# Freeing the accumulator banks of two kinds of fill earlier in the slot, and moving a ScalarE cast, in a fused cross-attention and spectral feed-forward layer

## The chip, the cores and the metric

The kernel runs on one core of one Trainium2 chip. The core has TensorE (PE, which multiplies matrices and turns tiles, and writes its results to eight PSUM banks), VectorE (DVE), ScalarE (ACT), GpSimd (POOL) and SyncE (SP, which here only issues DMAs). Each engine works through its own instructions in the order in which they are written, and engines wait for one another through semaphores. The metric is the time of one execution on the device in microseconds (us).

## The reference

Two sequences of 2048 tokens with 512 channels go through one attention layer over 128 context tokens and one feed-forward layer in the frequency domain.

```
def attention(decoder_output, encoder_output, mask, ...):      # 16 heads of 32 channels
    q = decoder_output @ wq_w + wq_b ;  k = encoder_output @ wk_w + wk_b ;  v = encoder_output @ wv_w + wv_b
    score = einsum('bhqd,bhkd->bhqk', q, k) / sqrt(32) * mask
    score = where(score == 0, -1e9, score)
    context = einsum('bhqk,bhkd->bhqd', softmax(score), v)
    return context @ wo_w + wo_b
def ffn(x, w_real, w_imag, bias):
    return real(ifft(fft(x) @ complex(w_real, w_imag))) + bias
x = x + attention(layernorm(x), ctx_1024, mask, ...)
x = x + ffn(layernorm(x), w_freq_real, w_freq_imag, bias)
```

## The kernel before

The spectral layer is folded into one real 512x512 matrix `M` while the kernel starts up. Matrices are split into a high and a low float16 part (`h` and `l`), and a product is made of three float16 matmuls.

**Chunks, slots and fills.** The 4096 tokens are 16 chunks of 256. For each chunk there are four steps of attention, one for each group of four heads, so 64 steps. All engines run a written-out software pipeline of *slots*: slot `v` (`V0` = 2 up to 79) holds the work of step `v` and, behind it by some slots, the later stages of earlier steps. In the text `r` is `v % 4`, and a slot with r = 1 is called an r1 slot. On DVE a slot begins with `mask_mul(v)` (scores times mask, read from the score banks), and then has `zero_to_neg(v)` and `least(v)` (the row minimum). GpSimd turns the minimum into the exponent's bias. ScalarE makes the exponentials of step v-1 in its slot `v`, in two halves, with `copy_pt` (the copies of the turned weights, which PE made by transposing the exponentials of step v-2) between them. PE runs `weigh` (weights times values, in even slots), `turn` (the transposes), then the slot's fills, then `scores(v+1)`, then late fills.

**Fills** are the matmul groups that share the three PSUM banks `G`. Fill number `n` uses bank `n % 3`, and PE may begin it only when fill `n-3` has been freed: `pe.wait_ge(g_free, n - 2)`. DVE raises `g_free`, one count a fill, strictly in the order of the fills' numbers, at the end of its `lo(n)`. The kinds of fill that matter here:

- `QQ`: half of a chunk's query projection, 24 matmuls. ScalarE casts the high part (`qh`, line 683), then DVE takes the low part (`ql`, line 862) and frees the bank. QQ with half 0 stands at the end of r3 slots, half 1 at the end of r1 slots.
- `R`: the reciprocals of the softmax sums, turned by four transposes, at the end of even slots. ScalarE copies them out (`rec`, line 725) at the head of the next slot; DVE only has to raise `g_free` with an empty instruction (line 847).
- `ST`: the token statistics of a coming chunk, two small transposes (line 462). ScalarE copies them out (`srow`, line 649), DVE again only raises `g_free` on line 847.
- `WO` (r0 and r1 slots) and `FF` (r2 and r3 slots): output projection and feed-forward, 12 matmuls each, read by DVE alone (lines 869 and 875).
- `U` and `M`: the pieces of the folded matrix, only in slots 4 to 11, with copies `od` on ScalarE (line 664) and sums on DVE (827, 832). `fold` on DVE (line 946) adds up pieces of the spectral matrix in slots 4 and 5.

A slot's fills in the plan are `mid` ones, ahead of the scores, and `late` ones behind them. ScalarE and DVE deal with the late fills of slot v-1 in slot `v`, as `held`. Both do so near the end of the slot's work: DVE behind `least(v)`, ScalarE behind both halves of the exponentials and `ctx_hi`:

```
for n in held + mids:
    lo(n)
```

In the steady stretch the order of fills is FF, QQ (r3 slot), WO, R, ST (r0 slot), WO, QQ (r1 slot), FF, R (r2 slot). So the QQ of the r1 slot takes the bank of the R of the r0 slot, and the ST takes the bank of the QQ of the r3 slot.

Of the kernel before, what the change touches and what calls it, by code (L numbers as in the profile page):

```python
# [17 lines left out]
NC = NB * S // CH  # L18
NS = 4 * NC
V0, V1 = 2, NS + 16  # L20
VS = 9
VP = 4
LAST = ("FF", NC - 1, 1)
NEG = 1e9
MASK_SCALE = 1e-9 / 32.0 ** 0.5 / 8.0
# [11 lines left out]
def plan():  # L37

    fills, slots, held = [], {}, []
    lead = [("W1", 0), ("CT", 0), ("CT", 1), ("K", 0), ("ST", 0), ("Q", 0, 0), ("Q", 0, 1), ("S", 0),
            ("W1", 1), ("Q", 0, 2), ("S", 1), ("K", 1), ("Q", 0, 3), ("ST", 1), ("Q", 1, 0), ("S", 2),
            ("Q", 1, 1), ("Q", 1, 2), ("Q", 1, 3)]
    front = []
    for f in lead:
        if f[0] == "S":
            front += [("S", f[1], 0), ("S", f[1], 1)]  # L50
        else:
            front.append(("G", len(fills)))
            fills.append(f)
    early = {
# [3 lines left out]
    }  # L58
    queries = {2: (2, 0), 4: (2, 1), 5: (3, 0), 6: (3, 1)}
    for v in range(V0, V1):  # L60
        c, r = divmod(v, 4)
        mid = {
            0: [("WO", c - 2, 0)],
            1: [("WO", c - 2, 1)],
            2: [("FF", c - 3, 0)],
            3: [("FF", c - 3, 1)],
        }[r]
        mid = [f for f in mid if 0 <= f[1] < NC] + early.get(v, [])
        if mid == [LAST]:
            mid = [LAST, (*LAST, "right")]  # L70
        late = []
        if v % 2 == 0 and 0 <= v - 4 < NS:
            late.append(("R", (v - 4) // 2))
        if v % 4 == 0 and 3 <= v // 4 + 2 < NC:
            late.append(("ST", v // 4 + 2))
        if v in queries:
            late.append(("QQ",) + queries[v])
        elif v >= 7 and v % 2 == 1 and (v + 9) // 4 < NC:
            late.append(("QQ", (v + 9) // 4, (v + 9) % 4 // 2))
        base = len(fills)  # L80
        fills += mid + late
        mids = list(range(base, base + len(mid)))
        lates = list(range(base + len(mid), len(fills)))
        items = []
        if v % 2 == 0 and 0 <= v - 4 < NS:
            items += [("PV", (v - 4) // 2)]
        if 0 <= v - 2 < NS:
            items += [("PT", v - 2, 0), ("PT", v - 2, 1)]
        items += [("G", n) for n in mids]
        if 0 <= v + 1 < NS:  # L90
            items += [("S", v + 1, 0), ("S", v + 1, 1)]
        items += [("G", n) for n in lates]
        slots[v] = (items, held, mids)
        held = lates
    return fills, front, slots


def stats_slot(c, t):
# [7 lines left out]
def hi_slot(c):  # L106
    return 5 if c == 4 else 4 * (c - 3)
# [11 lines left out]
def build(nc, x, xt, ctx_in, mask, wq, bq, wk, bk, wv, bv, wo, bo, lparts, tables, bf, eye, sums, pick, places, heads, out):  # L119
    fills, front, slots = plan()  # L120
    at = {f: n for n, f in enumerate(fills)}

    with ExitStack() as stack:
# [148 lines left out]
        def columns(n):  # L272

            if fills[n] == LAST:
                return slice(0, 256)
            return slice(256, 512) if fills[n][:3] == LAST else slice(0, 512)

# [365 lines left out]
        def _(act):  # L643
# [59 lines left out]
            def exps(s, t):  # L703
                if t == 0:
                    act.wait_ge(p_nb, s + 1)
                for j in range(4):
                    z = zs[:, s % NZ, t, j, :]
                    i = 4 * t + j
                    last = act.activation(z, z, ACT.Exp, bias=nbias[:, s % 4, i:i + 1], scale=-NEG,  # L709
                                          accum_out=zsum[:, s % 4, i:i + 1])  # L710
                if t == 1:
                    last.then_inc(ex_done, 1)

            def copy_pt(s, f):
                act.wait_ge(pt_done, 2 * s + f + 1)
                if f == 0 and s >= 2:
                    act.wait_ge(pv_done, s // 2)
                act.copy(pt[:, s % 2, 2 * f:2 * f + 2, :], PB[f][:]).then_inc(pt_copied, 1)  # L718

            def copy_rec(m):  # L720
                n = at["R", m]
                act.wait_ge(g_done, n + 1)
                if m >= 1:
                    act.wait_ge(cn_done, m)
                act.copy(rec[:], G[n % 3][:].rearrange("p (i n) -> p i n", i=2)).then_inc(rc_done, 1)

            def ctx_hi(m):
                c, h = divmod(m, 2)
                act.wait_ge(cn_done, m + 1)
                if h == 0 and c >= 2:  # L730
                    act.wait_ge(g_done, at["WO", c - 2, 1] + 1)
                act.copy(ch[:, c % 2, 2 * h:2 * h + 2, :], cn[:]).then_inc(ch_done, 1)
# [37 lines left out]
            hi(at["Q", 1, 3])  # L770
            for v in range(V0, V1):
                c, r = divmod(v, 4)
                held, mids = slots[v][1:]
                if v % 2 == 1 and 0 <= v - 5 < NS:
                    copy_rec((v - 5) // 2)
                if 2 <= v - 1 < NS:
                    exps(v - 1, 0)
                if 0 <= v - 2 < NS:
                    copy_pt(v - 2, 0)
                    copy_pt(v - 2, 1)  # L780
                if v == 2:
                    act.wait_ge(d_wo, 16)
                    act.activation(wos[:], wos[:], ACT.Identity, scale=SO).then_inc(w_sc, 1)
                    act.wait_ge(w_sc, 1)
                    act.copy(woh[:], wos[:]).then_inc(w_hi, 1)
                if 2 <= v - 1 < NS:
                    exps(v - 1, 1)
                if v % 2 == 1 and 0 <= v - 5 < NS:
                    ctx_hi((v - 5) // 2)
                if 0 <= v - 9 < 4:  # L790
                    high_m(v - 9)
                for n in held:
                    hi(n)
                if v == 3:
                    split_hi(3)
                for n in mids:
                    hi(n)
                if r == 1 and 0 <= c - 2 < NC:
                    norm_hi2(c - 2, 0)
                if r == 2 and 0 <= c - 2 < NC:  # L800
                    norm_hi2(c - 2, 1)
                for a in range(4, NC):
                    if hi_slot(a) == v:
                        split_hi(a)
        @block.vector
        def _(dve):
# [103 lines left out]
            def ctx_norm(m):  # L910
                dve.wait_ge(rc_done, m + 1)
                if m >= 1:
                    dve.wait_ge(p_cl, m)
                dve.tensor_tensor(cn[:], CX[:].rearrange("p (i n) -> p i n", i=2), rec[:], ALU.mult).then_inc(cn_done, 1)  # L914
# [100 lines left out]
            lo(at["Q", 1, 3])  # L1015
            for v in range(V0, V1):
                c, r = divmod(v, 4)
                held, mids = slots[v][1:]
                if 0 <= v < NS:
                    mask_mul(v)  # L1020
                if v % 2 == 1 and 0 <= v - 5 < NS:
                    ctx_norm((v - 5) // 2)
                if 0 <= v < NS:
                    zero_to_neg(v)
                if 0 <= v < NS:
                    least(v)
                if 0 <= v - 9 < 4:
                    low_m(v - 9)
                for n in held + mids:
                    lo(n)  # L1030
                tasks = []
                tasks += [(stats1, mean1, a, t) for a in range(4, NC) for t in range(2) if stats_slot(a, t) == v]
                if r == 0 and 0 <= c - 2 < NC:
                    tasks.append((stats2, mean2, c - 2, 0))
                if r == 1 and 0 <= c - 2 < NC:
                    tasks.append((stats2, mean2, c - 2, 1))
                for stats, _, *ct in tasks:
                    stats(*ct)
                if v % 2 == 1 and 0 <= v - 3 < NS:
                    recip((v - 3) // 2)  # L1040
                for _, mean, *ct in tasks:
                    mean(*ct)
                if c - 2 == NC - 1 and r < 2:
                    last_lo2(r)
                if v in (4, 5):
                    for n in range(3 * v - 6, 3 * v - 3):
                        fold(n)

        @block.gpsimd
        def _(pool):  # L1050
# [155 lines left out]
            for v in range(V0, V1):  # L1206
                c, r = divmod(v, 4)
                if v == 8:
                    constant_row()
                if v == VP:  # L1210
                    spread(0)
# [43 lines left out]
                for a in (3, 4):  # L1255
                    if lo_slot(a) == v:
                        split_lo(a)
                if v > VP and v % 2 == 1 and 0 <= v - 3 < NS:
                    spread((v - 3) // 2)
# [100 lines left out]
```

## Time and profile before

| | |
|---|---|
| median of 3 runs | 487.33 us (487.2 to 487.72) |
| the profiled execution's own time | 487.75 us |
| its span, first to last instruction | 486.0 us |
| PE busy | 441.3 us (91%) |
| DVE busy | 403.6 us (83%) |
| ACT busy | 366.8 us (75%) |
| POOL busy | 349.3 us (72%) |

Busy time is the time in which an engine has at least one instruction under way. The ends of matmuls are modelled and neighbours overlap, so a PE that is busy is not at its peak. Idle time counts only where it holds up the chain of work that ends last.

### The profile page before, as it was taken

To read this page: it belongs to the slowest core of one execution; us is meant where nothing else is said; L and a number is where in the kernel's file an instruction comes from. 1 tells how busy PE (TensorE), PEld (TensorE's weight loads), DVE (VectorE), ACT (ScalarE), POOL (GpSimd) and SP (SyncE) were. 2 spreads that over 40 slices of the span, in tenths; PEclk is the share of its full clock that TensorE was granted. 3 is DMA by queue.
4 is the path that set the end of the run, shared out by engine and by line. 5 is a ranking of instruction groups with operands and counts; after the bars stand their busy time and mean duration, and the time that the engine had idled before them with its cause. 6 is when DMAs were issued, how large, how long until landed. Compare 5 with 4: busy or idle time off the path is not lost.

```text
span 486.0 us, 10923 instructions
## 1 busy us (share of the span) xinstructions
PE 441.3 (91%) x3510; PEld 298.5 (61%) x3510; DVE 403.6 (83%) x538; ACT 366.8 (75%) x1342; POOL 349.3 (72%) x476
## 2 busy tenths in 40 slices
PE   7989859968889898989898999989898989989897
PEld 5777647747566565656565656666565665655444
DVE  3797589867989898898989898989899888999543
ACT  3358757757978888878979888888888879989810
POOL 6579552853867969696969697887969776865663
PEclk9999999979999999999999999999999999999999
DMA  8995834223415355454445353535442333321334
GB/s 285 394 349 142 289 110 107 66 59 86 90 48 143 101 142 113 129 128 117 108 128 118 85 128 103 146 99 141 104 101 70 93 75 83 76 58 30 88 98 120
DMA packets 85286, 60.15 MB, mean 124 GB/s; under 512 B 40141, under 2 KB 72813, under 8 KB 84718
## 3 DMA queue, kind: packets, MB, share of 16 engines
q1 hardware_dynamic: 84508, 59.29, 45.5%
q8 instruction: 29, 0.48, 0.4%
q10 hardware_dynamic: 722, 0.17, 0.2%
q14 instruction: 27, 0.22, 0.1%
HBM read 29.33 MB, written 8.39 MB: 78 GB/s over the span
## 4 chain that ended last, share of the span: by engine, by line
PE 49%; DVE 24%; ACT 10%; issue 10%; DMA 3%; SPq 2%; POOL 1%; DVEq 0%; ACTq 0%; POOLq 0%
PE bank L454 16%; PE bank L449 16%; DVE zs L897 7%; ACT zs L709 6%; PE bank L606 6%; PE bank L620 5%; DVE nmin L902 4%; DVE zs L890 3%; DVE cn L914 2%; PE scores L594 2%; ACT pt L718 2%; DVE st L971 2%; DVE x L869 2%; SPq L287 2%; DMA cxs<-in_ctx 2%
## 5 line engine op out<-in xcount | busy, mean ns | idle before, releaser
L709 ACT ACTIVATE zs<-zs,nbias 128x128 f32<-128x128 f32 x512 | 199.5, 395 | 18.6 <-POOL nbias L1124 18.3
L718 ACT COPY pt<-bank 128x512 f32<-128x512 f32 x128 | 67.9, 581 | 41.5 <-PE bank L606 41.5
L709 ACT ACTIVATION_READ_ACCUMULATOR zs<-zs,nbias 128x1 f32 x512 | 98.5, 192 | 0.0
L897 DVE SCALAR_TENSOR_TENSOR zs<-zs 128x1024 f32<-128x1024 f32 x64 | 88.7, 1386 | 1.2
L902 DVE TENSOR_REDUCE nmin<-zs 128x8 f32<-128x1024 f32 x64 | 78.1, 1220 | 2.2
L454 PE MATMUL bank<-xth,wqh 128*128 128x256 f16 x224 | 61.5, 275 | 19.4 <-DVEq L847 16.6
L890 DVE TENSOR_TENSOR zs<-scores,ms 128x1024 f32<-128x1024 f32 x64 | 78.1, 1220 | 1.1 <-issue 0.6
L1084 POOL TENSOR_TENSOR xs<-xs,bob 128x512 f32<-128x512 f32 (+1 forms) x41 | 42.8, 1046 | 48.4 <-DVE zs L897 44.0
L606 PE MATMUL bank<-ident,zs 128*128 128x128 f32 x512 | 68.3, 276 | 1.9 <-ACT zs L709 1.9
L606 PEld LDWEIGHTS bank<-ident,zs 128*128 128x128 f32 x512 | 55.7, 140 | 15.3 <-issue 10.7
L454 PE MATMUL bank<-xth,wql 128*128 128x256 f16 x224 | 61.2, 273 | 0.0
L454 PE MATMUL bank<-xtl,wqh 128*128 128x256 f16 x224 | 61.2, 273 | 0.0
L449 PE MATMUL bank<-woh,ch 128*128 128x512 f16 x128 | 48.5, 379 | 2.9 <-POOL cl L1137 2.1
L449 PE MATMUL bank<-wol,ch 128*128 128x512 f16 x128 | 48.5, 379 | 0.0
L449 PE MATMUL bank<-woh,cl 128*128 128x512 f16 x128 | 48.5, 379 | 0.0
L449 PE MATMUL bank<-mh,x1h 128*128 128x512 f16 x120 | 45.5, 379 | 0.0
L449 PE MATMUL bank<-ml,x1h 128*128 128x512 f16 x120 | 45.5, 379 | 0.0
L449 PE MATMUL bank<-mh,x1l 128*128 128x512 f16 x120 | 45.5, 379 | 0.0
L1124 POOL TENSOR_SCALAR nbias<-nmin 128x8 f32<-128x8 f32 x64 | 15.8, 247 | 36.3 <-issue 18.9
L594 PEld LDWEIGHTS scores<-ks,qs 102*128 102x128 f16 (+1 forms) x480 | 32.1, 98 | 14.7 <-DVE zs L890 1.4
L1110 POOL TENSOR_TENSOR x<-x,bfb 128x512 f32<-128x512 f32 x32 | 40.7, 1274 | 0.0
L862 DVE TENSOR_TENSOR ql<-bank,qh 128x512 f16<-128x512 f32 x28 | 19.3, 691 | 25.4 <-ACT qh L683 24.3
(126 smaller groups left out, 950.6 us busy)
## 6 DMA issues: line engine op xcount, KB each, us to landing
xs<-in_x SPq DMA_DIRECT2D x16, 512.0 KB, 4.3
xtr<-in_xt SPq DMA_DIRECT2D x16, 512.0 KB, 4.5
out<-x SPq DMA_DIRECT2D x31, 256.0 KB, 2.5
qs<-qh SPq DMA_DIRECT2D x120, 64.0 KB
lp<-in_lparts SPq DMA_DIRECT2D x4, 1024.0 KB, 9.3
qs<-ql SPq DMA_DIRECT2D x60, 64.0 KB
ms<-in_mask SPq DMA_DIRECT2D x16, 128.0 KB, 2.5
wqs<-in_wq SPq DMA_DIRECT2D x2, 512.0 KB, 7.0
```

The lines of the kernel that those rows point to most:

```text
L449: last = pe.matmul(o, a, b, start=(i == 0), stop=(i == len(mm) - 1))
L454: last = pe.matmul(o, a, b, start=(first and i == 0), stop=(i == len(pairs) - 1))
L594: last = pe.matmul(A[:, n % 2, 128 * j:128 * j + 128], qs[c % 2][0:rows, g, j, 128 * t:128 * t + 128], ks[0:rows, g, j, c // (NC // NB), : ...
L606: last = pe.transpose(PB[f][:, a:a + 128], zs[:, s % NZ, t, 2 * f + i, :], ident[:])
L620: last = pe.matmul(CX[32 * j:32 * j + 32, 256 * i:256 * i + 256], vs[:, b, n:n + 32], pt[:, i, j, :], start=True, stop=True)
L709: last = act.activation(z, z, ACT.Exp, bias=nbias[:, s % 4, i:i + 1], scale=-NEG, accum_out=zsum[:, s % 4, i:i + 1])
L718: act.copy(pt[:, s % 2, 2 * f:2 * f + 2, :], PB[f][:]).then_inc(pt_copied, 1)
L890: dve.tensor_tensor(zs[:, s % NZ], A[:].rearrange("p t (h k) -> p t h k", h=4), ms[:, c % NM].unsqueeze(2).broadcast_to([128, 2, 4, KEYS]) ...
L897: dve.scalar_tensor_tensor(out=z, in0=z, scalar=0.0, in1=z, op0=ALU.is_equal, op1=ALU.subtract).then_inc(eq_done, 1)
L902: dve.tensor_reduce(nmin[:, s % 4, :], zs[:, s % NZ].rearrange("p t h k -> p (t h) k"), AX.X, ALU.min).then_inc(mn_done, 1)
L1084: i = pool.tensor_tensor(z, z, bob[:, n], ALU.add)
L1110: pool.tensor_tensor(z, z, bfb[:], ALU.add).then_inc(p_x1b, 1)
```

## The change

Three things are rearranged; no arithmetic is added or removed.

1. In the plan, ST of chunk `a` moves one slot ahead, from the end of slot 4a-8 (r0, behind R) to slot 4a-9 (r3, ahead of QQ). ST of chunk 3 moves from slot 4 to slot 3, and ST of chunk 4 from slot 8 to slot 10.
2. The late fills of a slot are divided in two lists. `prompt` (R and ST) is dealt with at the head of the next slot: on ScalarE ahead of the first exponentials, on DVE between `mask_mul`/`ctx_norm` and `zero_to_neg`. `held` (QQ) stays behind `least` on DVE.
3. On ScalarE, from slot `VQ` = 6 on, the cast of a held QQ stands between the first half of the exponentials and `copy_pt`.

```diff
+VQ = 6
@@ plan
-        if v % 4 == 0 and 3 <= v // 4 + 2 < NC:
-            late.append(("ST", v // 4 + 2))
+        late += [("ST", a) for a in range(3, NC) if row_slot(a) == v]
@@
-        slots[v] = (items, held, mids)
+        slots[v] = (items, [n for n in held if fills[n][0] in ("R", "ST")],
+                    [n for n in held if fills[n][0] not in ("R", "ST")], mids)
@@
+def row_slot(c):
+
+    return {3: 3, 4: 10}.get(c, 4 * c - 9)
@@ ScalarE
-                held, mids = slots[v][1:]
+                prompt, held, mids = slots[v][1:]
                 if v % 2 == 1 and 0 <= v - 5 < NS:
                     copy_rec((v - 5) // 2)
+                for n in prompt:
+                    hi(n)
                 if 2 <= v - 1 < NS:
                     exps(v - 1, 0)
+                if v >= VQ:
+                    for n in held:
+                        hi(n)
                 if 0 <= v - 2 < NS:
                     copy_pt(v - 2, 0)
                     copy_pt(v - 2, 1)
@@
-                for n in held:
-                    hi(n)
+                if v < VQ:
+                    for n in held:
+                        hi(n)
@@ VectorE
                 if 0 <= v < NS:
                     mask_mul(v)
                 if v % 2 == 1 and 0 <= v - 5 < NS:
                     ctx_norm((v - 5) // 2)
+                for n in prompt:
+                    lo(n)
                 if 0 <= v < NS:
                     zero_to_neg(v)
```

**PE, steady stretch.** The line numbers of the changed kernel are up to 12 higher. Before, at the end of an r0 slot PE has the scores, the R transposes (`rzb`), then the ST transposes (`stok`), and then the next slot's turn:

```order
L449 MATMUL bank<-woh,cl 128x512
L594 MATMUL scores<-ks,qs_63 128x128 x8
L555 MATMUL bank<-ident,rzb 128x128 x4
L462 MATMUL bank<-ident_56,stok 128x128 x2
L606 MATMUL bank<-ident,zs 128x128 x8
```

After, ST stands at the end of an r3 slot, between the scores and the 24 matmuls of QQ:

```order
L455 MATMUL bank<-mh,x1l 128x512
L600 MATMUL scores<-ks,qs_64 128x128 x8
L468 MATMUL bank<-ident_56,stok 128x128 x2
L460 MATMUL bank<-xth,wqh 128x256
L460 MATMUL bank<-xth,wql 128x256
L460 MATMUL bank<-xtl,wqh 128x256
```

The order of fills is now FF, ST, QQ (r3), WO, R (r0), WO, QQ (r1), FF, R (r2). The QQ of the r1 slot takes the bank of the WO of the r0 slot, the ST that of the FF of the r2 slot, and the QQ of the r3 slot that of the R of the r2 slot.

**DVE, an r1 slot before.** The two empty instructions that free R and ST (`ISA x2`) stand behind `least`, ahead of the WO sum:

```order
L890 TENSOR_TENSOR zs<-scores,ms 128x1024
L914 TENSOR_TENSOR cn<-bank,rec 128x512
L897 SCALAR_TENSOR_TENSOR zs<-zs 128x1024
L902 TENSOR_REDUCE nmin<-zs 128x8
L847 ISA x2
L869 SCALAR_TENSOR_TENSOR x_76<-bank,xs 128x512
L971 BN_STATS st_101<-x_76 128x6
```

After, these are an r0 slot, which now frees ST behind `mask_mul`, and the r1 slot behind it, which frees R behind `ctx_norm`:

```order
L902 TENSOR_TENSOR zs<-scores,ms 128x1024
L859 ISA
L909 SCALAR_TENSOR_TENSOR zs<-zs 128x1024
L914 TENSOR_REDUCE nmin<-zs 128x8
L874 TENSOR_TENSOR ql<-bank,qh 128x512
L881 SCALAR_TENSOR_TENSOR x_76<-bank,xs 128x512
L983 BN_STATS st_101<-x_76 128x6
L988 BN_AGGR ag_102<-st_101 128x2
L902 TENSOR_TENSOR zs<-scores,ms 128x1024
L926 TENSOR_TENSOR cn<-bank,rec 128x512
L859 ISA
L909 SCALAR_TENSOR_TENSOR zs<-zs 128x1024
```

Both frees moved ahead of `zero_to_neg` and `least`, and that of ST one slot ahead as well.

**ScalarE, an r0 slot before.** The cast of QQ (`qh`) stands behind both halves of the exponentials:

```order
L709 ACTIVATE zs,zsum<-zs,nbias 128x128 x4
L718 COPY pt<-bank 128x512 x2
L709 ACTIVATE zs,zsum<-zs,nbias 128x128 x4
L683 CAST qh<-bank 128x512
L694 CAST xth<-xtr 128x1024
L725 COPY rec<-bank 128x512
```

After, the copy of ST (`srow`) opens the slot and the cast of QQ stands ahead of the copies of the turned weights:

```order
L655 CAST srow<-bank 64x256
L715 ACTIVATE zs,zsum<-zs,nbias 128x128 x4
L689 CAST qh<-bank 128x512
L724 COPY pt<-bank 128x512 x2
L715 ACTIVATE zs,zsum<-zs,nbias 128x128 x4
L700 CAST xth<-xtr 128x1024
L731 COPY rec<-bank 128x512
```

Nothing moved on GpSimd and SyncE.

## Rows read from the trace of the kernel before

**Rows 1.** Windows: length, busy PE, PEld, DVE, ACT, POOL; granted clock; DMA.

```profile
60.00:110.00 50.00, 40.15 (x312) 31.36 (x309) 40.39 (x59) 32.95 (x122) 27.22 (x40) 0.93 0.33 88
240.10:266.10 26.00, 24.53 (x202) 16.35 (x202) 23.49 (x30) 21.94 (x84) 21.12 (x30) 1.00 0.51 128
```

**Rows 2.** Waits of PE from 108 to 460 us: total, times, longest.

```profile
PE bank L454 <- DVEq L847: 16.6, 11, 1.6
PE bank L449 <- POOL cl L1137: 2.1, 3, 0.7
PE bank L462 <- DVE ql L862: 1.4, 1, 1.4
```

**Rows 3.** Timeline of PE, fills: start, us, instruction, [idle before <-releaser].

```profile
135.80 0.28 PE L454 MATMUL bank<-xth,wqh 128*128 128x256 f16 x1 [1.50 <-DVEq L847]
...
396.23 0.28 PE L454 MATMUL bank<-xth,wqh 128*128 128x256 f16 x1 [1.49 <-DVEq L847]
```

**Rows 4.** Timeline of DVE in one chunk of the steady stretch.

```profile
240.53 0.69 DVE L869 SCALAR_TENSOR_TENSOR x<-bank,xs 128x512 f32<-128x512 f32 x1 [0.49 <-ACT srow L649]
...
247.66 0.69 DVE L862 TENSOR_TENSOR ql<-bank,qh 128x512 f16<-128x512 f32 x1 [1.56 <-ACT qh L683]
...
249.75 1.22 DVE L890 TENSOR_TENSOR zs<-scores,ms 128x1024 f32<-128x1024 f32 x1
250.89 0.68 DVE L914 TENSOR_TENSOR cn<-bank,rec 128x512 f32<-128x512 f32 x1
```

**Rows 5.** Timeline of PE in the same chunk.

```profile
248.26 1.04 PE L606 MATMUL bank<-ident,zs 128*128 128x128 f32 x8
249.13 0.38 PE L449 MATMUL bank<-mh,x1h 128*128 128x512 f16 x1
...
251.72 0.61 PE L594 MATMUL scores<-ks,qs 102*128 102x128 f16 x8
```

**Rows 6.** Timeline of ScalarE: head and copies of an r0 slot, copies and cast of an r2 slot.

```profile
226.96 0.61 ACT L732 CAST ch<-cn 128x512 f16<-128x512 f32 x1
228.29 0.40 ACT L709 ACTIVATE zs<-zs,nbias 128x128 f32<-128x128 f32 x1 [0.72 <-POOL nbias L1124]
...
230.56 1.08 ACT L718 COPY pt<-bank 128x512 f32<-128x512 f32 x2 [0.61 <-PE bank L606]
...
244.54 1.07 ACT L718 COPY pt<-bank 128x512 f32<-128x512 f32 x2 [2.02 <-PE bank L606]
...
247.05 0.57 ACT L683 CAST qh<-bank 128x512 f16<-128x512 f32 x1
```

**Rows 7.** Part 5 of the page: `zero_to_neg`, busy, mean ns | idle before.

```profile
L897 DVE SCALAR_TENSOR_TENSOR zs<-zs 128x1024 f32<-128x1024 f32 x64 | 88.7, 1386 | 1.2
```

**Rows 8.** Timeline of DVE: one of the longest `zero_to_neg`.

```profile
411.17 1.98 DVE L897 SCALAR_TENSOR_TENSOR zs<-zs 128x1024 f32<-128x1024 f32 x1
```

**Rows 9.** Timeline of PE, fills of slots 4, 5, 9 and 11.

```profile
62.95 0.28 PE L454 MATMUL bank<-xth,wqh 128*128 128x256 f16 x1 [2.00 <-DVE us L827]
69.83 1.99 PE L454 MATMUL bank<-tb,lp 128*128 128x256 f32 x8 [3.22 <-DVEq L847]
103.45 3.78 PE L454 MATMUL bank<-tb,us 128*128 128x256 f32 x8 [3.78 <-DVEq L847]
117.27 1.99 PE L454 MATMUL bank<-tb,us 128*128 128x256 f32 x8 [0.61 <-DVE ql L862]
```

**Rows 10.** Waits of DVE from 62 to 120 us.

```profile
DVE mf L832 <- ACT od L664: 4.4, 2, 3.7
DVE ml L881 <- ACT mh L688: 3.8, 2, 3.0
DVE ql L862 <- ACT qh L683: 2.5, 4, 1.3
DVE us L827 <- ACT od L664: 1.5, 1, 1.5
```

**Rows 11.** Timeline of DVE, the mask multiply of slot 6.

```profile
75.38 1.22 DVE L890 TENSOR_TENSOR zs<-scores,ms 128x1024 f32<-128x1024 f32 x1
```

More of the change, by code:

```diff
@@ L1017, in _ @@
                 c, r = divmod(v, 4)
-                held, mids = slots[v][1:]
+                prompt, held, mids = slots[v][1:]
                 if 0 <= v < NS:
```

## The prediction

> **What bounds the kernel now.** I read the page first: PE is the busiest engine, and the chain that ended last runs through it for half of the span, but DVE is a close second. So I went to the windows. In one chunk of the steady stretch, 26.00 us long, PE is busy 24.53, DVE 23.49, ScalarE 21.94 and GpSimd 21.12 us, at full clock [rows 1]. No other engine is busy as long as PE, and 26.00 less 24.53 leaves 1.5 us in which PE stands still. The view of waits says for what: 16.6 us in 11 waits for DVE's line 847, which is the empty instruction that frees the bank of an R or an ST [rows 2]. The timeline of PE has the first of them at 135.80 and the last at 396.23, each 1.5 us ahead of the first matmul of a QQ [rows 3]. The reader is to see two things there. The waits are (396.23 - 135.80) / 10 = 26.04 us apart, one for each chunk, so this is the period of the whole stretch. And it is the QQ of an r1 slot, which takes the bank of the R of the r0 slot. That R had been copied out by ScalarE long before; DVE frees it only behind `zero_to_neg` and `least` of the r1 slot. It is a wait for a formality.
>
> Ahead of this stretch, from 60 to 110 us, PE is busy 40.15 of 50 us and its granted clock is 0.93 [rows 1]. Three fills of slots 4 to 9 waited 2.00, 3.22 and 3.78 us; the last of these, eight matmuls of M, then took 3.78 us where eight of the same shape took 1.99 in slot 11 [rows 9]. The ratio of 1.9 is the lower of TensorE's two clocks (1.2 against 2.4 GHz), behind an idle time of 3.78 us.
>
> **The change in the steady stretch.** The QQ of r1 now takes the bank of the WO of the r0 slot, which DVE frees at the end of its r0 slot, ahead of the mask multiply of the r1 slot; and PE comes to the QQ only behind scores that wait for that mask multiply. So the bank can't be late. The 1.50 us go, and the question is only what is late next. If PE never waits, the period is 26.04 - 1.50 = 24.54 us. The ST transposes are the same number of matmuls in another place and cost nothing new.
>
> Could DVE hold that? Its two waits in a chunk are 0.49 us for `srow` and 1.56 us for `qh` [rows 4]; there is no other above 0.3 us, so its work with the small gaps is 26.02 - 2.05 = 23.97 us. Both waits are ones that the change takes away. `srow` is copied a slot earlier. And `qh` of the r1 slot's QQ was cast only behind ScalarE's copies, which themselves had waited 2.02 us for PE, late by its own 1.50 us, and behind half of the exponentials, at 247.05 [rows 6]; now it is cast before those copies, in the time in which ScalarE waits for the turns. So DVE gains 2.05 us where PE gains 1.50. It is 0.57 us a chunk short of being the bound.
>
> The closest passes, each with PE moved by 1.50 and DVE by 2.05 us, where before and after is from the same chunk [rows 4, 5]. The scores at 251.72 need `mask_mul` of 249.75 to be done: 250.22 against 248.92, 1.3 us to spare. The FF at 249.13 takes the bank of the QQ whose low part ends at 248.35: 247.63 against 246.30, 1.3 us. The QQ of the r3 slot, right behind those scores and ST (some 0.6 us), now takes the bank of an R, freed behind `cn` at 251.57: about 250.8 against 249.5, 1.3 us. The turn at 248.26 needs the exponentials that ended when the cast at 247.05 began [rows 6]; both move by 1.50, and 1.2 us are left. None is under 1 us, so I expect no wait of PE in this stretch.
>
> ScalarE's cast ahead of the copies costs 0.57 us of its time at a place where it waits for the turns, 0.61 us in an r0 slot and 2.02 us in an r2 slot, of which 0.5 are left after the change [rows 6]. That covers it both times, just. Were the cover gone, the cast would put the copies off by 0.57 us and the turn's 1.2 us would still hide it. The copy of ST at the head of an r0 slot falls between 227.57, the end of the cast of `ch`, and 228.29, where ScalarE starts on the exponentials after a wait of 0.72 us for the bias [rows 6]. It is hidden as well.
>
> Eleven chunks have the wait: 11 x 1.50 = 16.5 us.
>
> **The change in the ramp (slots 3 to 12).** In slot 4 the QQ now takes the bank of the ST(3) of slot 3, freed behind `mask_mul(4)`: 2.00 us go. In slot 5 the U takes the bank of the U of slot 4, free for long: 3.22 go. That is 5.2 us, but DVE, busy with its folds, does not follow: in slot 5 it has only 1.5 us of waiting for `od` and 0.4 of the 2.5 for `qh` to lose [rows 10], so `mask_mul(6)`, which ended at 76.60 [rows 11], ends at 74.7. PE gives back about 2.8 us in slot 6 (behind that mask multiply, and for the low part of the slot's first query fill) and is 2.4 us ahead. Up to slot 8 the rest of the 2.5 us for `qh` goes and keeps it there. In slot 9 the M no longer waits for an R (3.78 us) and stays at the full clock (3.78 - 1.99 = 1.79 us). DVE's own waits for `od` and `mh` of M, 4.4 and 3.8 us [rows 10], were a result of this; I take 6.5 us of these 8.2, because each sum of M must still wait for ScalarE's casts, one after the other. That puts DVE 2.4 + 6.5 = 8.9 us ahead in slot 12. PE also loses 1.4 us anew in slot 10, where ST(4) now waits for the QQ of slot 9, and gains the 1.4 us that ST had waited in slot 12 for a low part [rows 2]. At the QQ of slot 13 I have PE 9.7 us ahead. This sum is the softest: its upper bound is all of PE's waits with the clock, 2.00 + 3.22 + 3.78 + 0.61 + 1.79 + 1.4 = 12.8 us [rows 2, 9]; its lower bound, if the later slots do not follow and only the first two waits go as far as DVE lets them, 2.4 us.
>
> **The end.** From slot 54 there is no QQ, and R stands without an ST; the banks' order there makes no wait before and none after. PE's other waits, 2.1 us for GpSimd's `cl` [rows 2], lie there. With ScalarE and GpSimd somewhat fuller I take 0.6 us more of them.
>
> Sum: 16.5 + 9.7 - 0.6 = 25.6 us. From the profiled execution's own 487.75 us (1.75 over its span of 486.0) that is 462.15. The median of the runs is 0.42 us lower: 461.7 us.
>
> **The rivals.** *The period does not reach PE's work, since DVE becomes the bound* (0.15). DVE has 0.57 us to spare and everything is packed closer. `zero_to_neg` takes 1386 ns in the mean [rows 7] and up to 1.98 us where GpSimd works beside it [rows 8]. If it took 0.3 us more in the mean, DVE's chunk would be 23.97 + 1.2 = 25.2 us, the gain 0.85 a chunk, the time 487.3 - 9.35 - 9.7 = 468.3. For it speaks that GpSimd is busy 21.12 of 26 us; against it that most of these overlaps are set by waits of GpSimd for `zero_to_neg` itself, which keep their place. If all four were at 1.98 us, the chunk would be 23.97 + 2.4 = 26.4 and the stretch gain nothing. The Trainium skill's page "SBUF — State Buffer" (section "Who interferes with whom") says that VectorE and GpSimd share one pair of ports as an exclusive lock, so that the loser stands still for the other's whole instruction. By that rule, the collisions are all or nothing, and the time of this rival is the one to expect as soon as one more `zero_to_neg` in a slot starts behind a GpSimd operation.
>
> *The ramp gives little* (0.10): PE keeps the order's new waits in slots 6 and 10, and a clock that falls once; 2.4 to 5 us instead of 9.7, time 466 to 469.
>
> *The wait is replaced by another of the same length* (0.03). It would be the ST or the QQ in the r3 slot waiting for R's free; I have 1.3 us to spare there. If ScalarE's copy of R came 2.8 us later than now, PE would wait 1.5 us at r3 in place of r1. Time: 487.3 - 9.7 = 477.6; with no gain in the ramp either, 487.
>
> *Slower: DVE held at the head of the r0 slot by the copy of ST* (0.02). DVE's empty instruction for ST waits for `srow`, ahead of `zero_to_neg`, and everything of the slot is queued behind it: `least`, the bias, the exponentials, the turns. ScalarE copies `srow` at the head of its slot, behind the cast of `ch`, which needs `cn`. DVE may wait there 2.05 us a chunk before the period is what it was, and 0.9 us more before the ramp's 9.7 us are used up too, so the kernel gets slower once `srow` comes 2.9 us behind `mask_mul`. At 3.3 us: 23.97 + 3.3 = 27.3 us a chunk, 487.3 - 9.7 + 11 x 1.25 = 491. Against it: ScalarE is through with `ch` at 227.57 and then idle until 228.29 [rows 6], so it has time to spare there as things are.
>
> **Chances and range.** 0.70 for the forecast, whose own range is 458 to 466 (ramp at its upper bound of 12.8 us, or some 4 us short in all). The range for 8 in 10 is 458 to 469, which takes in the first rival's time and the second's. A measurement of this kernel tells about 0.2% from no change. Faster 0.96, within 0.2% 0.01, slower 0.03.
>
> **What would show it.** In the trace after: no wait of PE for line 859 (847 before) in the steady stretch, chunks 24.5 us apart, PE busy 24.5 of them; DVE without the two waits for `srow` and `qh`; ScalarE's `copy_pt` still waiting for PE; the M of slot 9 at 2 us and a granted clock of 1.00 from 60 to 110 us. The forecast is wrong if DVE has no waits at all and PE waits for its mask multiply or its sums; if it is `srow`, the last rival holds.

## The result, and the profile after

The changed kernel takes 457.9 us (median of 4 runs, 457.34 to 458.18), the kernel before 487.29 us. The ratio is 0.9394, with a 95% interval of 0.9378 to 0.9410. The forecast was 461.7 us with a range of 458 to 469, so the time lies just under the range: 25.6 us were forecast and 29.4 came. The profiled execution took 458.18 us, its span is 456.4 us.

The span is 29.6 us shorter. In it DVE and ScalarE are busy for as long as before, GpSimd for 5.5 us more (354.8 against 349.3) and PE for 6.4 us less. This is the first part of the page after:

```profile
span 456.4 us, 10923 instructions
PE 434.9 (95%) x3510; PEld 297.5 (65%) x3510; DVE 403.8 (88%) x538; ACT 366.7 (80%) x1342; POOL 354.8 (78%) x476
```

The windows after, of the ramp (the same 60 to 110 us as in [rows 1]), of one chunk between the scores of two r2 slots, and of the steady stretch (columns as in [rows 1]):

```profile
60.00:110.00 50.00, 45.08 (x376) 35.72 (x374) 46.59 (x68) 39.73 (x147) 32.25 (x44) 1.00 0.32 88
276.82:301.02 24.20, 24.20 (x204) 16.37 (x203) 23.58 (x31) 21.88 (x83) 21.36 (x30) 1.00 0.49 119
120.00:370.00 250.00, 249.42 (x2087) 168.57 (x2085) 242.28 (x311) 225.98 (x850) 217.22 (x297) 1.00 0.49 120
```

The chunk takes 24.20 us and PE is busy in all of it. The granted clock in the ramp is 1.00, where it was 0.93. From 120 to 370 us the waits of PE and DVE have only these rows:

```profile
PE bank L455 <- DVE ql L874: 0.6, 1, 0.6
...
DVE x L881 <- PE bank L455: 1.9, 1, 1.9
DVE x L887 <- PE bank L455: 0.3, 2, 0.2
DVE zs L902 <- PE bank L612: 0.3, 1, 0.3
DVE zs L902 <- issue: 0.3, 1, 0.3
```

No wait for the empty instruction is left (line 859, once 847), and none of DVE for `srow` or `qh`. ScalarE's timeline in that chunk has the copy of ST, the cast and the copies of an r0 slot, then the cast and the copies of an r2 slot:

```profile
282.95 0.37 ACT L655 CAST srow<-bank 64x256 f16<-64x256 f32 x1
...
284.77 0.57 ACT L689 CAST qh<-bank 128x512 f16<-128x512 f32 x1
...
286.15 1.07 ACT L724 COPY pt<-bank 128x512 f32<-128x512 f32 x2 [0.81 <-PE bank L612]
...
297.36 0.56 ACT L689 CAST qh<-bank 128x512 f16<-128x512 f32 x1
...
298.19 1.07 ACT L724 COPY pt<-bank 128x512 f32<-128x512 f32 x2 [0.27 <-PE bank L612]
```

Both times ScalarE still waits for PE's turns behind the cast, 0.81 and 0.27 us: the cast is hidden, as it was put.

**Where the 29.4 us came from.** PE's scores mark the same point of the program in both traces. Before, those of steps 14, 55 and 63 begin here:

```profile
133.69 0.61 PE L594 MATMUL scores<-ks,qs 102*128 102x128 f16 x8
...
403.48 0.61 PE L594 MATMUL scores<-ks,qs 102*128 102x128 f16 x8
...
444.67 0.61 PE L594 MATMUL scores<-ks,qs 102*128 102x128 f16 x8
```

After, they begin here:

```profile
123.97 0.62 PE L600 MATMUL scores<-ks,qs 102*128 102x128 f16 x8
...
373.60 0.61 PE L600 MATMUL scores<-ks,qs 102*128 102x128 f16 x8
...
415.10 0.61 PE L600 MATMUL scores<-ks,qs 102*128 102x128 f16 x8
```

The lead is 9.72 us at step 14, right ahead of the QQ of slot 13; 29.88 at step 55, behind all eleven waits; and 29.57 at step 63. So the ramp gave 9.7 us, the steady stretch 20.16 and the end took back 0.3. (The profiled execution after had been 0.33 us behind at the scores of step 3, 44.43 against 44.10, ahead of any change; the ramp itself gave 10.0.)

**What the wait really cost.** Before, the scores, R, ST and turn of an r0 slot, the scores and the waiting QQ of an r1 slot, and the scores and the QQ of an r3 slot, which does not wait, begin here on PE:

```profile
233.83 0.61 PE L555 MATMUL bank<-ident,rzb 128*128 128x128 f32 x4
234.42 0.28 PE L462 MATMUL bank<-ident,stok 128*128 128x128 f16 x2
234.54 1.04 PE L606 MATMUL bank<-ident,zs 128*128 128x128 f32 x8
...
238.01 0.61 PE L594 MATMUL scores<-ks,qs 102*128 102x128 f16 x8
...
240.12 0.28 PE L454 MATMUL bank<-xth,wqh 128*128 128x256 f16 x1 [1.50 <-DVEq L847]
...
252.17 0.27 PE L454 MATMUL bank<-xth,wqh 128*128 128x256 f16 x1
```

From the scores at 238.01 to the QQ at 240.12 are 2.11 us; the first and the last of these waits are in [rows 3]. Between the scores at 251.72 [rows 5] and the QQ at 252.17 are 0.45 us. The wait cost 1.66 us, not the 1.50 that stands in its row as idle time: the row counts from the modelled end of the last matmul, and in an unbroken stream the next group begins 0.16 us ahead of that end. The second part stands in no row of PE's matmuls. R at 233.83 and ST at 234.42 are 0.59 us apart, while behind an R without an ST the next group begins after 0.44 (289.43 and 289.87 after). PE is listed as busy in between, since R's modelled end is 234.44. The wait falls on the weight load of ST (PEld, which runs ahead of the matmul), and the view of waits has it there. From 130 to 380 us, of the kernel before and then of f1 (below), whose R alone is freed early:

```profile
PEld bank L462 <- DVE ql L862: 3.7, 10, 1.7
```

```profile
PEld bank L462 <- DVE ql L862: 2.3, 10, 0.4
```

In every chunk ST's weight load waits for the low part of the QQ whose bank it takes. (Of the 3.7 us before, 1.7 are the one in slot 12.) Kernels f2, f3 and f4 and the changed kernel have no such row in that stretch, and f5 has it once, with 0.3 us. After:

```profile
281.18 0.61 PE L600 MATMUL scores<-ks,qs 102*128 102x128 f16 x8
281.63 0.28 PE L468 MATMUL bank<-ident,stok 128*128 128x128 f16 x2
281.74 0.27 PE L460 MATMUL bank<-xth,wqh 128*128 128x256 f16 x1
...
289.43 0.61 PE L561 MATMUL bank<-ident,rzb 128*128 128x128 f32 x4
289.87 1.04 PE L612 MATMUL bank<-ident,zs 128*128 128x128 f32 x8
```

ST costs 0.11 us there and nobody waits. 1.66 + 0.15 = 1.81 us a chunk; measured from scores to scores, a chunk went from 26.02 to 24.19 us, 1.83.

### The profile page after: what moved, and what is told of

The parts are those of the page before. It is cut to its first block, busy times and chain, and to the rows that moved or that the text cites. A ratio compares the mean times of both kernels' runs of the same rounds, so it can differ in the third digit from the quotient of the medians.

```text
span 456.4 us, 10923 instructions
## 1 busy us (share of the span) xinstructions
PE 434.9 (95%) x3510; PEld 297.5 (65%) x3510; DVE 403.8 (88%) x538; ACT 366.7 (80%) x1342; POOL 354.8 (78%) x476
## 4 chain that ended last, share of the span: by engine, by line
POOL 40%; issue 19%; PE 17%; DVE 13%; ACT 5%; DMA 3%; SPq 2%; ACTq 1%; POOLq 0%; DVEq 0%
PE bank L455 9%; POOL xs L1098 7%; POOL rzb L1145 6%; POOL cl L1151 5%; POOL x L1124 4%; POOL xtl L1089 4%; PE bank L460 4%; ACT zs L715 3%; DVE zs L909 3%; POOL ve L1105 3%; POOL x1nl L1113 3%; DVE zs L902 2%; SPq L293 2%; POOL nbias L1138 2%; POOL ms L1131 2%
## 5 line engine op out<-in xcount | busy, mean ns | idle before, releaser
L909 DVE SCALAR_TENSOR_TENSOR zs<-zs 128x1024 f32<-128x1024 f32 x64 | 90.3, 1412 | 1.2
L1151 POOL TENSOR_TENSOR cl<-cn,ch 128x512 f16<-128x512 f32 x32 | 37.6, 1174 | 6.0 <-ACT ch L738 5.6
L1145 POOL COPY rzb<-rz 128x512 f32<-128x512 f32 x32 | 40.0, 1251 | 2.4 <-DVE rz L920 2.4
```

The source lines that it names most:

```text
L909: dve.scalar_tensor_tensor(out=z, in0=z, scalar=0.0, in1=z, op0=ALU.is_equal, op1=ALU.subtract).then_inc(eq_done, 1)
L1145: pool.tensor_copy(rzb[:].rearrange("p i h w -> p (i h) w"), rz[:, z, :].rearrange("p i h -> p (i h)").unsqueeze(2).broadcast_to([128, 16, ...
L1151: pool.tensor_tensor(cl[:, c % 2, 2 * h:2 * h + 2, :], cn[:], ch[:, c % 2, 2 * h:2 * h + 2, :], ALU.subtract).then_inc(p_cl, 1)
```

## The experiments

Each kernel was timed in three rounds beside the kernel before, on the same chip. The periods are mine, from the starts of PE's scores of steps 19 and 51, eight chunks apart: 26.05 us before, 24.19 after. (One chunk before is 0.24 us longer than the others' 26.02.)

| kernel | median us | ratio to before, 95% interval | period us |
|---|---|---|---|
| the change | 457.9 | 0.9394 (0.9378 to 0.9410) | 24.19 |
| f1: R freed at the head alone | 462.03 | 0.9465 (0.9445 to 0.9484) | 24.37 |
| f2: cast moved alone | 480.69 | 0.9849 (0.9832 to 0.9866) | 25.37 |
| f3: change without the cast's move | 457.58 | 0.9384 (0.9360 to 0.9407) | 24.19 |
| f4: change with ST in its old slots | 458.66 | 0.9399 (0.9382 to 0.9415) | 24.20 |
| f5: f1 and f2 together | 461.31 | 0.9464 (0.9419 to 0.9509) | 24.26 |
| g1: change, 0.11 us more on DVE a slot | 457.84 | 0.9400 (0.9362 to 0.9439) | 24.19 |
| g2: change, 0.27 us more on DVE a slot | 457.61 | 0.9394 (0.9357 to 0.9431) | 24.19 |
| g3: change, 0.49 us more on DVE a slot | 463.95 | 0.9491 (0.9465 to 0.9518) | 24.86 |
| h1: change, three folds to GpSimd | 458.75 | 0.9422 (0.9382 to 0.9461) | 24.19 |
| h5: change, QQ of slot 4 early too | 458.16 | 0.9377 (0.9350 to 0.9403) | 24.19 |
| h4: h1 and h5 together | 456.14 | 0.9332 (0.9306 to 0.9358) | 24.19 |
| h2: change, ST(4) in slot 8 | 457.9 | 0.9368 (0.9337 to 0.9399) | 24.19 |

The kernel before had medians of 487.3 to 489.3 us beside these (single runs of 484.7 to 489.7, with a mean granted clock of 0.996 to 0.989), so small differences are read within a group that was timed together: f1 to f4; f5, g1, g2 and h1; g3, h5, h4 and h2. The change itself was timed in none of the three groups. Where it is compared with them, the period and the starts of PE's scores, counted from step 4, decide.

**f1: only the free of R.** On DVE, in the kernel before:

```diff
+                for n in held:
+                    if fills[n][0] == "R":
+                        lo(n)
                 if 0 <= v < NS:
                     zero_to_neg(v)
...
                 for n in held + mids:
-                    lo(n)
+                    if fills[n][0] != "R":
+                        lo(n)
```

> The kernel before, with one thing changed: DVE frees R's bank at the head of the next slot. ST and ScalarE's cast stay where they were. Theory A (the wait of 1.5 us a chunk was all that held PE, and its real cost is read from one start to the next: the scores at 238.01 and the QQ at 240.12 are 2.11 us apart where the same pair without a wait, 251.72 and 252.17, is 0.45 apart, so 1.66 us, not 1.50): the period falls from 26.04 to 24.38 us, 11 x 1.66 = 18.3 us, and the ramp gives some 8 us since U and M of slots 5 and 9 no longer wait for an R; about 461 us. Theory B (the free alone uncovers DVE's wait for the cast of qh, so that the cast's move is needed for most of the gain): the period falls by no more than 0.9 us and the time is 467 to 472 us.

It took 462.03 us, with a period of 24.37 us. Theory A holds to 0.01 us in the period, and its time is missed by 1 us. One empty instruction, moved ahead of two others, is worth 1.67 us a chunk and 26.0 us in all; f3, the change without the cast's move, gains 30.4 us in the same group. The period also bears out that the wait's price is to be read from start to start: 1.66 us were read so, and 1.67 came.

**f2: only the cast.**

```diff
                     exps(v - 1, 0)
+                if v >= 6:
+                    for n in held:
+                        if fills[n][0] == "QQ":
+                            hi(n)
                 if 0 <= v - 2 < NS:
                     copy_pt(v - 2, 0)
...
                 for n in held:
-                    hi(n)
+                    if v < 6 or fills[n][0] != "QQ":
+                        hi(n)
```

> The kernel before, with only the cast of QQ on ScalarE moved ahead of the copies, from slot 6 on. Theory A: the QQ of r1 still waits for DVE's least, but DVE is earlier there, since its wait of 1.56 us for qh goes; it can use only the part up to the end of the FF matmuls, 247.5 against 248.26, so 0.75 us a chunk, period 25.3 us, with 1 to 2 us of the ramp: about 477.5 us. Theory B (the cast is only a cover, PE's wait stays at 1.5 us): 486 to 487.3 us.

It took 480.69 us, 7.3 us less than the kernel before beside it. That is less of a gain than theory A's 477.5, and far from B's. The waits of PE and DVE from 150 to 400 us show where it went:

```profile
PE bank L454 <- DVEq L852: 10.0, 10, 1.2
...
DVE x L880 <- PE bank L449: 8.6, 10, 1.0
DVE x L874 <- ACT srow L649: 6.5, 10, 0.7
```

PE's wait for R's free shrank from 1.50 to 1.00 us a chunk, and the 0.15 us of ST's weight load went; most chunks are 0.68 us shorter (26.02 to 25.34). DVE lost its wait for `qh` but now waits 0.86 us for the FF matmuls in its place, and 0.65 instead of 0.49 for `srow`. So the period is 25.37, not the 25.3 of my sum, and the ramp gave about nothing: M of slot 9 still waits for its R there. The cast is one link of the same chain that f1 cuts at another place.

**f3: the change without the cast's move.** `VQ = 999`.

> The changed kernel, with the cast of QQ put back behind both halves of the exponentials in all slots. Theory A: DVE's wait for qh in the r2 slot comes back, but PE keeps 0.8 us to spare at the scores and at the FF that need DVE, so the period stays at 24.19 us; the ramp loses up to 1.5 us: 458 to 459.5 us. Theory B (cast needed): DVE's wait of about 1.5 us a chunk makes DVE the bound, period 24.9 us or more, 465 us or more.

457.58 us, period 24.19: theory A, without the loss in the ramp that it allowed for. DVE waits again (0.3 us a chunk), and PE does not care:

```profile
DVE ql L874 <- ACT qh L689: 3.0, 8, 1.4
```

Once R and ST are both freed at the head, the cast's move is worth nothing on top. The change has two remedies for one wait, and the early frees are the full one.

**f4: ST in its old slots.** `return 4 * c - 8`, still copied and freed at the head.

> The changed kernel, with ST back in its old slots (4a-8, behind R) and still dealt with at the head of the next slot. Theory A: in the steady stretch ST's old place cost its wait for the bank of a QQ, some 0.17 us a chunk (from the R at 233.83 to the turn at 234.54 are 0.71 us, of which R takes 0.44 and ST 0.11), and with DVE as early as it now is that low part is written before PE comes there, so the period stays at 24.19 to 24.3 us; the ramp loses slot 4's 2.00 us wait but DVE bounds it there anyway, and it no longer has the wait of 1.66 us for ST in slot 10: 457 to 459.5 us. Theory B (ST's move gives 0.17 us a chunk and the 2 us of slot 4): 461.5 to 463 us.

458.66 us, period 24.20: theory A. The 0.15 us did not belong to ST's place. They were the wait for the low part, which DVE now writes in time. The move of ST itself is worth at most 1 us, in the ramp.

**f5: f1 and f2 together.**

> The kernel before with R's bank freed at the head and the cast of QQ ahead of the copies; ST in its old slots, freed and copied as before. Theory A (the 0.18 us a chunk between 24.37 us with R's free alone and 24.19 us with the whole change is ST's wait for the low part of a QQ, which DVE writes earlier once it has no wait for qh): the period is 24.2 us, the time 459.5 to 461 us. Theory B (the 0.18 us belong to ST's place behind R): the period stays at 24.37 us, 461.5 to 462.5 us.

461.31 us, with a period of 24.26 us: between theory A (24.2 us, 459.5 to 461 us) and theory B (24.37 us). Of the ten chunks five take 24.19 to 24.21 us, four 24.25 to 24.27 and one 24.47. The 0.15 us go in half of the chunks: with ST copied and freed late, DVE is still sometimes late with the low part. That supports A as to what ST waited for. It also shows that the cast's move alone does not keep the wait away in all chunks; f3 and f4, where ST is dealt with at the head, have 24.19 and 24.20 us.

**g1, g2, g3: how near DVE is.** In slots 14 to 53, behind `least(v)`:

```diff
+                if 14 <= v < 54:
+                    dve.memset(kh[:].rearrange("p g b k -> p (g b k)")[:, 0:128], 0.0)
```

with 128, 512 and 1024 elements of a tile that is no longer used.

> The changed kernel with one small memset more on DVE in each of the slots 14 to 53 (128 elements a partition, of a tile no longer used; some 0.1 us each with its gap, 0.4 to 0.5 us a chunk). Theory A (DVE is right behind PE: in a chunk of 24.2 us it is without work only 0.25 us): the period rises by 0.15 to 0.3 us, the time by 2 to 3 us, to 460 to 461 us. Theory B (PE alone is the bound, with 0.6 us a chunk or more of room on DVE): no change, 457.5 to 458.5 us.

> As the last one, with 512 elements (0.3 to 0.48 us each, 1.2 to 1.9 us a chunk). Theory A: the period is DVE's work, 24.0 us and the memsets, 25.2 to 25.9 us, and the time rises by 10 to 17 us. Theory B: by 0.6 us a chunk less, 6 to 11 us.

Neither did anything: 457.84 and 457.61 us. For g1 that is theory B. For g2 both theories fell, since B too had expected 6 us or more: with 0.25 us a chunk in which DVE was seen to wait, four memsets of 272 ns should have cost some 0.8 us. The groups by line of DVE tell why, of the change and of g2, both from 150 to 340 us:

```profile
L909 DVE SCALAR_TENSOR_TENSOR zs<-zs 128x1024 f32<-128x1024 f32 x31 | 44.4, 1433 | 0.5
```

```profile
L909 DVE SCALAR_TENSOR_TENSOR zs<-zs 128x1024 f32<-128x1024 f32 x31 | 40.9, 1320 | 0.5
...
L1042 DVE MEMSET kh<- 128x256 uint32 x32 | 8.7, 272 | 0.1
```

`zero_to_neg` became 113 ns shorter in the mean, 0.45 us a chunk, and the FF sums 61 ns (745 to 684), 0.12 us a chunk. The rest came out of waits and gaps: DVE's busy time in these 190 us rose only from 185.21 to 187.22 us.

Why `zero_to_neg` shrinks can be read from the traces. Two of GpSimd's operations after, and the two `zero_to_neg` that begin while they are under way:

```profile
285.37 0.74 POOL L1098 TENSOR_TENSOR xs<-xs,bob 128x256 f32<-128x256 f32 x1
...
296.85 1.29 POOL L1124 TENSOR_TENSOR x<-x,bfb 128x512 f32<-128x512 f32 x1
```

```profile
285.40 1.79 DVE L909 SCALAR_TENSOR_TENSOR zs<-zs 128x1024 f32<-128x1024 f32 x1
...
292.49 1.22 DVE L909 SCALAR_TENSOR_TENSOR zs<-zs 128x1024 f32<-128x1024 f32 x1
...
297.69 1.53 DVE L909 SCALAR_TENSOR_TENSOR zs<-zs 128x1024 f32<-128x1024 f32 x1
```

GpSimd's operations end 0.71 and 0.45 us after the start of `zero_to_neg`, which takes 1.79 and 1.53 us: 1.08 us more than what was left of them, both times. At 292.49 only 0.02 us of an operation were left, and it took 1.22. The same sum, 1.09 us and the rest of GpSimd's operation but never less than 1.22 us, gives 61 of the 64 `zero_to_neg` after within 0.04 us, and 59 of the 64 before. In the few others the operation under way held `zero_to_neg` up less, or not at all. In g2 the `zero_to_neg` of the same place in the chunk begins later against the same GpSimd operation. Of that 0.43 us are left, and it takes 1.52 us in place of 1.79:

```profile
285.08 0.73 POOL L1100 TENSOR_TENSOR xs<-xs,bob 128x256 f32<-128x256 f32 x1
```

```profile
285.38 1.52 DVE L909 SCALAR_TENSOR_TENSOR zs<-zs 128x1024 f32<-128x1024 f32 x1
```

So, with these few exceptions, a `zero_to_neg` that begins behind a GpSimd operation stands still until that ends, and work put ahead of it takes up this standing time first. That part of DVE's busy time is elastic.

> As the two memset runs before it, with 1024 elements (about 0.54 us each). With 0.27 us each the period stayed at 24.19 us: DVE's net load of 0.8 us a chunk was taken up by its 0.25 us without work and by shorter collisions of zero_to_neg (mean 1329 ns instead of 1436). Theory A (with that DVE was just full, so each further microsecond counts): 4 x 0.27 = 1.1 us a chunk more, period 24.9 to 25.3 us, time 465 to 468 us. Theory B (DVE still has room of its own, or the memset runs beside other work): period 24.2 to 24.4 us, below 460 us.

463.95 us, period 24.86 us: a little under theory A's 24.9 us and 465 us, far from B's. Here DVE is the bound. From 150 to 340 us it has no wait at all, and PE's weight loads wait for its `mask_mul` (5.7 us in 15 waits) and for its low part (3.8 us in 8). `zero_to_neg` is down to 1252 ns and has little left to give:

```profile
L909 DVE SCALAR_TENSOR_TENSOR zs<-zs 128x1024 f32<-128x1024 f32 x31 | 38.8, 1252 | 0.5
...
L1042 DVE MEMSET kh<- 128x512 uint32 x31 | 15.0, 485 | 1.7
```

Between g2 and g3 the memsets grew by 4 x 0.21 = 0.85 us a chunk and the period by 0.66. So DVE's real room beside PE is what g2 loads (4 x 0.27 us, some of which lies over its neighbours in time) and about 0.2 us more.

**h1, h5, h4, h2: what holds the ramp now.** In the trace after, PE's fills of slot 6 wait 1.37 and 1.35 us, and ST in slot 10 waits 1.66:

```profile
73.69 1.97 PE L460 MATMUL bank<-tb,lp 128*128 128x256 f32 x8 [1.37 <-issue]
...
77.89 0.28 PE L460 MATMUL bank<-xth,wqh 128*128 128x256 f16 x1 [1.35 <-DVE ql L874]
...
83.13 0.61 PE L600 MATMUL scores<-ks,qs 102*128 102x128 f16 x8
...
108.16 0.28 PE L468 MATMUL bank<-ident,stok 128*128 128x128 f16 x2 [1.66 <-DVE ql L874]
```

h1 moves the three folds of slot 5 from DVE to GpSimd, with a semaphore of their own:

```diff
-                if v in (4, 5):
-                    for n in range(3 * v - 6, 3 * v - 3):
+                if v == 4:
+                    for n in range(6, 9):
                         fold(n)
...
                     spread(0)
+                    for n in range(9, 12):
+                        fold(n, l_top, n - 9)
```

> The changed kernel with DVE's three folds of slot 5 (2.4 us) moved to GpSimd, ahead of its work of slot 4, where it stood idle for 3.2 us. Nothing else changed. Theory A (in slots 5 and 6 of the ramp it is DVE that holds PE back, through its folds and the mask multiply behind them): PE's waits in slots 6 (1.37 and 1.35 us) shrink and the time falls by 1 to 2 us, to 456 to 457 us. Theory B (ScalarE's casts and the exponentials are the limit there, or GpSimd's bias comes later by as much): within 0.5 us of 457.9.

458.75 us, outside both theories: no gain, and rather a loss of 1 us against g1 and g2 beside it. The wait in its trace names what I had not counted, the DMAs that stack chunk 2's queries:

```profile
83.66 0.55 PE L602 MATMUL scores<-ks,qs 102*128 102x128 f16 x7 [2.26 <-DMA qs<-srow]
```

h5 leaves the folds and deals with the QQ of slot 4 early, so that these DMAs start earlier:

```diff
-VQ = 6
+VQ = 5
...
+                if v == 5:
+                    prompt, held = prompt + held, []
                 for n in prompt:
                     lo(n)
```

> The changed kernel, with the query fill of slot 4 dealt with early as well: ScalarE casts it ahead of the copies in slot 5, DVE takes its low part at the head of slot 5. The stacking DMAs of chunk 2 then start 2.4 us earlier. Theory A (in the ramp DVE's sum of work in slots 4 to 7 is the limit, and the DMAs are only just in time): no gain, 457.4 to 458.3 us. Theory B (the DMAs hold the scores of step 8): 1 us or more gained, 456.9 us or less.

458.16 us, no gain: theory A. In its trace the scores of step 8 begin 27.76 us behind those of step 4, after the change 27.39. The DMAs are not the limit while DVE is. h4 has both edits:

> The last one with DVE's folds of slot 5 on GpSimd too. With the folds moved alone, PE's scores of step 7 came 1.1 us earlier but those of step 8 then waited 2.3 us for the stacking DMAs. Theory A (DVE and the DMAs are the two limits of the ramp, one right behind the other): both together gain 1.2 to 1.8 us, 456.1 to 456.7 us. Theory B (a third limit is as close): 457.4 us or more.

456.14 us, 2.0 us less than h5 beside it, and the fastest kernel of the study. The scores of step 8 begin at 81.17:

```profile
81.17 0.61 PE L602 MATMUL scores<-ks,qs 102*128 102x128 f16 x8
```

That is 2.0 us ahead of 83.13, and 1.7 us if both are counted from the scores of step 4. Two limits lay one right behind the other; either alone gives nothing.

h2 puts ST(4) back in slot 8 (`{3: 3, 4: 8}`).

> The changed kernel with ST of chunk 4 in slot 8, behind R, where it was before, all else as changed. Theory A (PE's new wait of 1.66 us for ST in slot 10 goes, but DVE and ScalarE, through the sums of M, set the pace of slots 9 to 12): less than 0.6 us gained or lost, 457.3 to 458.5 us. Theory B (PE's waits there count in full): 456.2 to 456.5 us.

457.9 us, against 458.16 of h5 beside it: theory A. The 1.66 us that PE waits in slot 10 cost nothing, since PE comes too early there. From the scores of step 4 to those of step 14 are 68.34 us here and 68.23 after the change. That DVE and ScalarE, with the sums of M, set the pace there fits this, but no run shows it by itself.

## Why the prediction was nearly right, and what was off

- **The wait and its cause:** right. All eleven waits went, and f1 shows that it was R's free behind `least` alone.
- **No new wait in the steady stretch:** right. PE is busy in 24.20 of 24.20 us. I had taken 1.2 to 1.3 us to spare at each of the closest passes, and none failed.
- **"11 x 1.50 = 16.5 us":** this is the step that failed, and by size only. The stretch gave 20.2 us. The term was taken from the idle time in the row, 1.50, where from start to start it is 1.66; and ST's delay of 0.15 us, which stands in no row of PE's waits, was left out ("the ST transposes ... cost nothing new"). 11 x 1.83 = 20.1 us. This term makes 3.7 of the 3.8 us between forecast and time, and the end the rest. The range had no bound for this term at all: its lower end had come from the ramp's upper bound.
- **"If PE never waits, the period is 26.04 - 1.50 = 24.54":** wrong for the same reason; 24.19. My own reading of 24.53 us busy in [rows 1] seemed to support it, but that too counts the modelled tail of the last matmul ahead of the wait, and the time in which ST's weight load waits behind R.
- **The ramp, 9.7 us:** right, 9.72 at the scores ahead of the QQ of slot 13, with the M of slot 9 at the full clock. The stages agree too: 2.49 us ahead at the scores of step 8 (forecast 2.4) and 8.83 at those of step 13 (forecast 8.9). The 0.8 us from 8.9 to 9.7 had no term of its own in the prediction. The traces have it: ST's wait of 1.44 us in slot 12 went, and a WO fill waits 0.58 us there instead. That the clock stayed up is seen: 1.00 in the window, and this M took 1.89 us. The new wait of ST in slot 10 came as well (1.66, forecast 1.4).
- **The end, 0.6 us lost:** 0.3, and not by more waits for `cl`, which stay at 2.1 us. It goes with the cast's move: from the scores of step 59 to those of step 63 are 21.57 to 21.58 us in the kernel before, f1 and f3, which cast late, and 21.84 to 21.87 us in all the others.
- **DVE "0.57 us a chunk short of being the bound":** g1 to g3 show more room than that, because `zero_to_neg` shrinks when DVE is loaded. The rival of a DVE bound through collisions did not occur: the mean rose from 1386 to 1412 ns [rows 7 have the first]. "All or nothing" was misread. The lock of the Trainium skill's page "SBUF — State Buffer" ("Who interferes with whom") agrees with these traces: the loser blocks while the other's instruction lasts. What is lost is then what is left of that instruction, so all values from 1.22 us up occur, up to the 1.98 us of [rows 8], where 0.90 us of a GpSimd operation were left. One more collision need not bring the time of that rival.

- **The slower rival:** ScalarE copied `srow` at 282.95 to 283.32, ahead of the end of DVE's mask multiply of that slot at 285.37. It never came near.

What stays open: how much of DVE's time could be won by ordering GpSimd's operations so that none is under way when a `zero_to_neg` begins. No run tried it.

## What to carry to other kernels

Read the price of a wait from the start of the group before to the start of the group behind it, against the same pair where nobody waits. The idle time in the row left out 0.16 us of 1.66 here, and a delay of 0.15 us that fell on a weight load was in no row of PE's matmuls, only in one of PEld; times eleven chunks that was 3.4 us. Read the waits of the weight loads too.

Where banks are freed in a fixed order, a fill whose data is long gone can still hold its bank, because its free stands behind work that it has nothing to do with. Here moving one such free was worth 26.0 us, where shortening the chain at the cast was worth 7.3, and with all such frees moved the cast's move added nothing.

When a limit is removed without gain, look in the trace for the one that took its place before giving it up: the folds alone lost about 1 us, the stacking DMAs alone gave nothing, and together they gave 2.0 us.

## What the hardware showed that I had not expected

DVE took up 272 ns more in each slot with no change of the time at all. In part that is because an instruction of its own shrank, from 1433 to 1320 ns in the mean, and to 1252 under the next load: when it begins during a GpSimd operation it lasts, in nearly all cases, 1.09 us and the rest of that operation, and otherwise 1.22 us. DVE was busy in 242.28 of 250 us, and still had more room than the 3% that this leaves: g2's memsets are 1.09 us in 24.19, 4.5%.
